# Mixture-of-experts stages of a nine-block hybrid: token scaling on ScalarE, every lower half on GpSimd, routing values in PSUM, and earlier events for the next block

## The reference

```python
def _ffn(x, router_W, router_b, sW1, sb1, sW2, sb2, eW1, eb1, eW2, eb2):   # E = 15, K = 3
    xt = x.reshape(n, d)                                   # x comes in layer-normed
    shared = relu(xt @ sW1 + sb1) @ sW2 + sb2
    probs = softmax(xt @ router_W + router_b)
    top_p, top_i = top_k(probs, K)
    cw = zeros((n, E)).at[arange(n)[:, None], top_i].set(top_p)
    h = relu(einsum('nd,edh->neh', xt, eW1) + eb1)
    ye = einsum('neh,ehd->ned', h, eW2) + eb2
    return shared + einsum('ned,ne->nd', ye, cw)

x = x + state_space(layernorm(x));      x = x + _ffn(layernorm(x), layer 0)
x = x + linear_attention(layernorm(x)); x = x + _ffn(layernorm(x), layer 0)
x = x + retention(layernorm(x));        x = x + _ffn(layernorm(x), layer 1)
x = x + softmax_attention(layernorm(x)); x = x + _ffn(layernorm(x), layer 1)
```

## Time and profile before

| what | value |
|---|---|
| median of 3 runs | 2277.0 us (2275.93 to 2284.58) |
| profiled execution | 2270.78 us, span of the core 2269.1 us |
| granted TensorE clock, mean over the span | 0.924 |
| busy share PE / DVE / ACT / POOL | 83% / 74% / 57% / 45% |
| a mixture stage, by windows of about its length | 230 to 234 us of each of the four |
| PE, DVE, ACT, POOL busy in ffn0a's 232 us | 202.1, 176.1, 162.0, 144.4 us |

### The profile page before, as it was taken

The page is one execution under the profiler, slowest core; times in us unless marked ns, Lnnn a source line. Parts: engine busy times, 40 slices in busy tenths (PEclk is TensorE's granted clock), DMA queues, the critical chain, the costliest instruction groups (busy, mean ns, idle before and its releaser), DMA issues. The chain is left out here.

```text
span 2269.1 us, 30482 instructions
## 1 busy us (share of the span) xinstructions
PE 1874.5 (83%) x9650; PEld 1290.2 (57%) x9650; DVE 1686.7 (74%) x4121; ACT 1289.0 (57%) x2199; POOL 1015.4 (45%) x948
## 2 busy tenths in 40 slices
PE   5886588888788876764588888999999999968888
PEld 3554477767577733332477765555555555537776
DVE  6997778766678779998577767776766767637776
ACT  3442377753577744443477764666665665556776
POOL 1110366652466632221466654534543544236666
PEclk8998799999899987776699999999999999979999
DMA  3000153310333310000233310000000000013332
GB/s 97 6 5 4 71 194 141 141 71 1 141 141 141 140 39 1 0 1 1 77 139 136 141 70 1 1 1 1 1 1 1 1 1 1 1 56 136 149 146 113
DMA packets 37075, 142.29 MB, mean 63 GB/s; under 512 B 6769, under 2 KB 18737, under 8 KB 24114
## 3 DMA queue, kind: packets, MB, share of 16 engines
q1 hardware_dynamic: 34608, 139.55, 15.7%
q10 hardware_dynamic: 2306, 0.78, 0.2%
HBM read 136.38 MB, written 3.93 MB: 62 GB/s over the span
## 5 line engine op out<-in xcount | busy, mean ns | idle before, releaser
L2312 ACT ACTIVATE soft_prob<-psum 128x1024 f32<-128x1024 f32 (+3 forms) x384 | 302.6, 813 | 203.7 <-PE psum L2192 202.2
L2404 DVE TENSOR_REDUCE soft_mx<-psum 128x1 f32<-128x512 f32 (+2 forms) x352 | 230.9, 687 | 116.1 <-PE psum L2262 79.4
L2262 PE MATMUL psum<-soft_own,soft_stack 128*128 128x512 f32 (+3 forms) x768 | 249.3, 376 | 24.6 <-DVE soft_mx L2400 11.0
L2192 PE MATMUL psum<-soft_stack,soft_own 128*128 128x512 f32 (+3 forms) x768 | 225.4, 377 | 2.8 <-POOL soft_stack L2169 2.2
L163 POOL TENSOR_TENSOR norm_rstd<-norm_mv,s_const_minus_half 128x4 f32<-128x4 f32 x64 | 65.1, 1018 | 350.2 <-DVE norm_mv L158 343.7
L2400 DVE CUSTOM_DVE_ANT_0 psum<-psum,s_soft_sel 128x384 f32<-128x384 f32 (+1 forms) x256 | 157.2, 638 | 65.1 <-PE psum L2262 64.4
L2192 PEld LDWEIGHTS psum<-soft_stack,soft_own 128*128 128x128 f32 x768 | 125.2, 189 | 133.0 <-issue 79.1
L2175 POOL TENSOR_SCALAR_AFFINE_SELECT soft_prob<-soft_prob 128x256 f32<-128x256 f32 x256 | 102.7, 408 | 203.8 <-ACT soft_prob L2312 200.9
L2262 PEld LDWEIGHTS psum<-soft_own,soft_stack 128*128 128x128 f32 x768 | 139.8, 192 | 92.6 <-DVE soft_mx L2404 42.8
L2209 PE MATMUL psum<-soft_prob,soft_v_pad 128*32 128x512 f32 (+3 forms) x1536 | 163.6, 498 | 3.5 <-ACT soft_prob L2312 2.1
L940 POOL TENSOR_TENSOR ffn1a_h_low<-ffn1a_t,ffn1a_h_high 128x512 fp32r<-128x512 f32 x96 | 128.2, 1351 | 72.7 <-ACT ffn1a_t L1064 70.5
(11 more groups left out here) (446 smaller groups left out, 5181.2 us busy)
## 6 DMA issues: line engine op xcount, KB each, us to landing
ffn0a_cw_all<-ffn0a_cw_dram SPq DMA_DIRECT2D x24, 1024.0 KB, 6.8
ffn0b_cw_all<-ffn0b_cw_dram SPq DMA_DIRECT2D x24, 1024.0 KB, 6.7
ffn1a_cw_all<-ffn1a_cw_dram SPq DMA_DIRECT2D x24, 1024.0 KB, 6.8
ffn1b_cw_all<-ffn1b_cw_dram SPq DMA_DIRECT2D x24, 1024.0 KB, 6.8
ffn0a_cw_all<-ffn0a_cw_dram SPq DMA_DIRECT2D x8, 768.0 KB, 10.5
ffn0b_cw_all<-ffn0b_cw_dram SPq DMA_DIRECT2D x8, 768.0 KB, 10.1
...
```

The costliest lines, as they stand in the source:

```text
L2192: ins = pe.matmul(e_ps[:, n % 2, j, low(n):BLK], own[:, u % 3, 2 * pair + j, kt * P:(kt + 1) * P], stack[:, u % HT, qb * BLK + low(n):(qb ...
L2262: ins = pe.matmul(per_head[:, n, :], stack[:, u % HT, i * P:(i + 1) * P], own[:, u % 3, g, half * BLK:half * BLK + width], start=(n == 0), ...
L2312: nc.scalar.activation(prob[:, done % PROBS, :, low(n):BLK], e_ps[:, n % 2, :, low(n):BLK], ACT.Exp, scale=float(HD) ** -0.5).then_inc(exp ...
L2404: nc.vector.tensor_reduce(mx[:, i, half, heads.start:heads.stop], bank[:, 0:width * len(heads)].rearrange("p (g k) -> p g k", k=width), AX ...
```

## The change

It touches only `ffn_stage`.

- `low_h` of all 128 steps is done by POOL; DVE's share, and the functions that dealt the steps out, are gone.
- The tokens are scaled by ACT: four activations `x * rstd + shift`. For that DVE also negates the mean (`aggregate(..., negate=True)`), and POOL's `invert` multiplies it with the inverse root into `shift`.
- `split_x` moves from POOL to DVE and reads the transposed tokens in PSUM. In the opening part of a stage DVE makes the lower halves of `w2`, which POOL made.
- `prob` lies in the router's PSUM bank, and so does the new `whole_ps`. `combine_weights` computes the same product four times, once into each place, where it had one product and two copies.
- The events of the next block come sooner: the statistics of block g + 2 at step 12 of block g, the scaling behind step 13, the copy behind step 15, and the transposes at step 1 of block g + 1 (they were at steps 0, 1, 1 and 3 of the block before the one prepared). Routing and its transposes stand two steps sooner.
- The first four experts' rows of block 0 are fetched by four DMAs of 256 KB in place of one of 1024 KB.

```diff
-        cwt_ps = logit_ps
+        prob, whole_ps, cwt_ps = logit_ps[:, :, 0:E + 8 - TOPK], logit_ps[:, :, 32:32 + E], logit_ps
...
+                if q == 0:
+                    for i in range(CHUNK_E):
+                        sp.dma_start(cw_all[:, 0, i, :], cw_dram[0, i:i + 1, :].to_broadcast([P, BLK]))\
+                            .then_inc(first_loaded[i], 16)
+                for c in range(q == 0, CHUNKS_E):
...
+            def invert(q):
+                norm.invert(pool, q)
+                pool.wait_ge(norm.rstd_ready, q + 1)
+                nc.gpsimd.tensor_tensor(shift[:, :], norm.mv[:, :, 0], norm.rstd[:, :], ALU.mult).then_inc(shift_ready, 1)
...
             if split:
-                low_weights("w1", w1_low, w1_high, slice(0, 4), 1, w1_ready)
-                low_weights("w2", w2_low, w2_high, slice(0, 4), 2, w2_ready)
-                low_weights("w1", w1_low, w1_high, slice(4, 8), 3, w1_ready)
-                low_weights("w1", w1_low, w1_high, slice(8, NE), 3, w1_ready)
-                low_weights("w2", w2_low, w2_high, slice(4, NE), 4, w2_ready)
...
+                low_w1(slice(0, 4), 1)
+                pool.wait_ge(cw_ready, 1)
+                low_w1(slice(4, 8), 2)
+            invert(1)
+            if split:
+                low_w1(slice(8, NE), 2)
+            for n in range(STEPS_ALL):
+                g, e = divmod(n, NE)
+                low_h(n)
+                if e == 11 and (g + 2 < BLOCKS or g + 2 == BLOCKS and out is None):
+                    invert(g + 2)
...
+            def scale(q):
+                act.wait_ge(shift_ready, q)
+                act.wait_ge(norm.xt_ps_ready, q)
+                for j in range(GT):
+                    ins = nc.scalar.activation(norm.xn[:, j, :], x[:, q % BLOCKS * GT + j, :], ACT.Identity,
+                                               scale=norm.rstd[:, j:j + 1], bias=shift[:, j:j + 1])
+                ins.then_inc(norm.xn_ready, 1)
...
-                link(nc.vector.scalar_tensor_tensor(cw_parts[:, p, :, B2_ROWS:B2_ROWS + E], left[:, :, 0:E], 0.0,
-                                                    prob[:, :, 0:E], ALU.is_lt, ALU.mult))
-                high, low = cw_parts[:, p, :, 0:NE], cw_parts[:, p, :, 32:32 + NE]
-                link(nc.vector.tensor_copy(high.bitcast(F32R), whole))
-                nc.vector.tensor_copy(cw_parts[:, p, :, 64:64 + NE], high)
-                nc.vector.tensor_tensor(low, whole, high, ALU.subtract).then_inc(cw_ready, 1)
+                at = cw_parts[:, p, :, :]
+                for part in (whole_ps, at[:, :, B2_ROWS:B2_ROWS + E], at[:, :, 0:E].bitcast(F32R),
+                             at[:, :, 64:64 + E].bitcast(F32R)):
+                    ins = nc.vector.scalar_tensor_tensor(part, left[:, :, 0:E], 0.0, prob[:, :, 0:E], ALU.is_lt, ALU.mult)
+                link(ins)
+                nc.vector.tensor_tensor(at[:, :, 32:32 + E], whole_ps, at[:, :, 0:E], ALU.subtract).then_inc(cw_ready, 1)
...
+            def split_x(q, p):
+
+                dve.wait_ge(norm.xt_ready, q + 1)
+                nc.vector.tensor_tensor(xt_parts[:, p, 1, :], norm.xt_ps[:, :, :].rearrange("p t k -> p (t k)"),
+                                        xt_parts[:, p, 0, :], ALU.subtract).then_inc(xt_split, 1)
```

More of the change, by code:

```diff
@@ L1028, in _ @@
             transpose_cw(0, 0)
+            norm.transpose(pe, 1)
             for n in range(H_BANKS, STEPS_ALL + LAG):
@@ L1092, in _ @@
                 halves(n)
-                if e == 1 and (g + 1 < BLOCKS):
-                    copy_x(g + 1, (g + 1) % 2)
-                if e == 1 and g + 1 == BLOCKS and out is None:
-                    norm.copy(act, BLOCKS, 0)
+                ahead = g + 2 < BLOCKS or g + 2 == BLOCKS and out is None
                 if e == 2 and g:
                     copy_y(g - 1)
-                if e == 4 and g + 1 < BLOCKS:
+                if e == 2 and g + 1 < BLOCKS:
                     exp(g + 1)
-                if e == 8 and g + 1 < BLOCKS:
+                if e == 6 and g + 1 < BLOCKS:
                     copy_cwt(g + 1, (g + 1) % 2)
+                if e == 13 and ahead:
+                    scale(g + 2)
+                if e == 15 and ahead:
+                    copy_x(g + 2, g % 2)
             copy_y(BLOCKS - 1)
@@ L1189, in _ @@
             combine_weights(0, 0)
+            statistics(1)
             if split:
@@ L1193, in _ @@
                                         ALU.subtract).then_inc(b2_ready, 1)
+                for i, highs in ((0, 3), (1, 4)):
+                    some = slice(W2_PIECES[i], W2_PIECES[i + 1])
+                    dve.wait_ge(w_high, highs)
+                    nc.vector.tensor_tensor(w2_low[:, some, :], w["w2"][:, some, :], w2_high[:, some, :],
+                                            ALU.subtract).then_inc(w2_ready, 1)
             for n in range(STEPS_ALL):
@@ L1197, in _ @@
                 weigh(n)
-                if n >= 2 and on_dve(n - 2):
-                    low_h(n - 2)
-                if e == 0 and (more or out is None):
-                    if not more:
-                        dve.wait_ge(x_done, 1)
-                    norm.statistics(dve, g + 1)
-                if e == 1 and (more or out is None):
-                    norm.scale(dve, g + 1)
+                if e == 1 and more:
+                    split_x(g + 1, (g + 1) % 2)
+                if e == 3 and more:
+                    shift_logits(g + 1)
                 if e == 4 and more:
-                    shift(g + 1)
+                    probabilities(g + 1)
                 if e == 5 and g:
                     add(g - 1)
+                if e == 5 and more:
+                    largest(g + 1)
                 if e == 6 and more:
-                    probabilities(g + 1)
-                if e == 7 and more:
-                    largest(g + 1)
-                if e == 8 and more:
                     combine_weights(g + 1, (g + 1) % 2)
-            low_h(STEPS_ALL - 1)
+                if e == 12 and (g + 2 < BLOCKS or g + 2 == BLOCKS and out is None):
+                    statistics(g + 2)
             add(BLOCKS - 1)
```

92 lines of the change are left out of this document (40 added, 52 removed).

## The result

The changed kernel takes 2133.07 us (median of four runs, 2130.68 to 2134.54). The kernel before, on the same chip, took 2279.3 us (2275.93 to 2284.58). The ratio is 0.9356, with a 95% interval from 0.9333 to 0.9378: 146 us, or 6.4%, less. The profiled execution took 2132.39 us.

The account below looks back on a forecast made before the run. The chain around a block, 24.85 us, was to bound, slightly over PE's 24.0. Blocks 97.8, first blocks 12 and openings 22.4, minus 2, give 130 less: 2270.8 becomes about 2141 profiled, 6.2 more as median: 2147, range 2108 to 2200.

Parts of the forecast that it names:

- main case: Mixture stages: a block takes 24.4 to 25.7 us, the kernel 2135 to 2166 us; chance 0.46.
- PE's own work: In a block: 16 steps at 1.36 us plus bias matmul, router and transposes, 24.0 us, unchanged by the edit.
- PE-bound: Rival, chance 0.25: the chain around a block closes under PE's 24.0 us, so a block costs 24.0; 2117 us.
- The chain of 24.85: Dependences once around a block, between transposes of combine weights, sum to 24.85 us; block 24.9, PE standing 0.9.
- Engine sums: Busy time per block after the change: POOL 21.5, ACT 21.6, DVE about 17.6 us, none above PE's 24.0.
- The wait for POOL: DVE's small instructions behind the statistics stand until POOL's lower half ends; L157 or L158 over 1 us in most blocks.
- PE's wait for scaled tokens: In a block, PE's stand until the next block's tokens are scaled: 2.81 us before, under 0.6 after.
- First blocks: Step 0 to step 15 of each stage's first block: 24.6 us against 27.9, rounded to 3.0 less each, 12 together.
- Openings: Opening parts of the four stages: 22.4 us less; first `weigh` about 7.7 us later, held by DVE's own work.
- Tails: Each stage's last lower half is now POOL's, not DVE's: 0.5 us lost each, 2 together.
- Slower rival: Chance 0.05: POOL's lower halves stretch to 1.87 us and bound a block at 31.1 us; about 2337 us.

Follow-up runs that it names:

- kernel with sooner statistics: Changed kernel with mean and variance in PSUM, plus statistics (step 10 instead of 12) and POOL's root and shift two steps sooner: 2133.25 us.
- the PSUM edit: Changed kernel with the next block's mean and variance aggregated into PSUM, so that DVE's two small operations read PSUM: 2128.12 us.
- the old times: Changed kernel with every event of the next block back at its old step, all else kept: 2216.76 us.
- kernel with the sooner transposes: Changed kernel with mean and variance in PSUM, statistics at step 10, and the first block's combine transposes ahead of PE's third expert of the opening: 2126.98 us.
- the kernel before with PSUM alone: Kernel before with only the routing values put in PSUM (five combine operations), all else and all times of before: 2257.55 us against 2273.23.
- the changed kernel without PSUM: Changed kernel with the routing values and whole combine weights back in SBUF, formed as before: 2153.53 us.

## Why the prediction came out as it did

The forecast was 2147, the time 2133, inside the range. The blocks are the main case's (24.4 to 25.7); the time is 2 us below that case's 2135 to 2166. Its sum was made against the span: 130 less, where 138.5 were measured. The other 5.5 us lie in the distance from the profiled execution to the median: 6.2 before, 0.7 after.

- **PE's own work.** I put it at 24.0 from the earlier trace rows. That window of 28.00 us isn't a block: it lies for the most part in one of 28.8 us and takes in that block's longer stand for the tokens (3.33 us, where most have 2.53), with 116 of a block's 117 matmuls. From one set of token transposes to the next (442.76 to 470.77) the kernel before takes 28.01 us, with 117 matmuls and stands of 2.53 and 0.96, which leaves 24.5. Measured after the change: 24.4, the same from two kernels (24.73 - 0.33 and 24.53 - 0.10). The rival "PE-bound" at 24.0 could not have come, but its mechanism did, at 24.4: PE is the limit, and the other engines' slack is real.
- **The chain of 24.85 was the step that failed.** It gave 24.9 us with PE standing 0.9. The block is 24.73, and PE stands 0.33. ACT idles 1.97 us within the drawn chain, and the kernel with sooner statistics kept the same block. The number was near by luck, because PE's work was set 0.4 too low and the stand 0.6 too high. What bounds is PE, and beside it one late lower half, not the chain around the block.
- **Engine sums.** POOL 21.5, ACT 21.6 and DVE 17.6 predicted; 21.5, 21.2 and 18.2 measured. DVE's excess is the negation's wait, which the PSUM edit turns into 17.1.
- **The wait for POOL** at L157 or L158 was predicted in most blocks and is there: 1178 ns at the median of L157. Its price for DVE was right, its price for the kernel is 0.2 us a block. I also said that the earlier trace rows show that routing values in PSUM don't meet POOL. They hold no such instruction; the runs do show it: 0.16 us for the negation from PSUM, 0.2 for the routing.
- **PE's wait for scaled tokens**, 2.81 in the earlier trace rows, is gone in the blocks. So is the second one, for the combine weights, 0.96 us in a block of 28.0, which I hadn't listed. I gave this to DVE's relief and the new places together. The runs part them: the old times cost 84 us, the scaling on DVE 67, a quarter of the lower halves 30 and the routing in SBUF 20. These are not shares, their sum is 201 for a gain of 146: each alone brings back a stand of PE.
- **First blocks.** 24.6 us each predicted, 22.7 measured: 19.9 less instead of 12. This is the largest mis-sized term, and it is PE's work in it. I had 15 whole steps, 20.4 us, and 1.5 of other work. From the first `weigh` to that of step 15 PE has 76 matmuls of 512 columns and not 90, because three `up` are done before it and `down` is four steps late: 17.3 us, and 1.9 for 12 others. The clock's start is there as I had it: 7 to 13 matmuls at 0.43 us apart, 1.8 us on average, at a granted clock of 0.81 to 0.85. The rest, about 1.6, is short waits, where I had 1.0. The window of ffn0b's first block:

```profile
537.20:560.50 23.30, 22.48 (x88) 18.63 (x89) 16.84 (x53) 16.04 (x30) 16.27 (x14) 0.81 0.65 249
```

- **Openings.** 22.4 predicted, 20.2 measured. The contention's part came as said (the products and the difference are done in 0.9 us). The reason for the rest was wrong: not DVE's own work holds the first `weigh`, it is free 4.5 us sooner. The slow third expert holds PE's transposes by 1.2 us, and copies, store and load follow. The kernel with the sooner transposes shows it. The cause of the gain was also told too simply: the kernel before with PSUM alone and the changed kernel without PSUM both have the short openings, so either of PSUM or POOL's new place is enough.
- **Tails.** I took off 2 us for the last lower halves; the part outside blocks and openings lost 3.6, mostly in the attention stage, whose time moves by as much between kernels that leave it alone.
- **Slower rival.** It rested on lower halves of 1.87 us. They took 1.30, as the argument against it said. The kernel before with all lower halves on POOL is slower by another way: 2%, by DVE's small instructions and not by POOL's pace.
